# Attention scores as plain fp32 matmuls on paired heads in place of stacked fp32r parts, with one pool of PSUM banks and a new order

## The reference, cut to what matters

```
scores = einsum('bqhd,bkhd->bhqk', q, k) / sqrt(8)    # q = h @ w_q + b_q, k = ctx @ w_k + b_k
attn   = softmax(scores)                              # windowed, full, or over the 16 best keys
o      = einsum('bhqk,bkhd->bqhd', attn, v)           # 16 heads of 8 features
x      = x + gate * (o @ w_o + b_o)
```

## Time and profile before

| what | value |
|---|---|
| runs | 824.49, 845.3, 851.21 us; median 845.3 |
| profiled execution | span 830.0 us from the first to the last instruction; its time outside the span is not listed |
| mean granted clock of TensorE | 0.751 of full speed |
| TensorE matmul busy | 694.1 us, 84% of the span, 5066 instructions |
| VectorE, ScalarE, GpSimd busy | 519.2, 405.8, 240.4 us |
| chain that ended last | TensorE 56%, VectorE 21%, GpSimd 7%, DMA 5% |

### The profile page before, as it was taken

How to read it: one execution, slowest core, us unless ns; L and a number is a source line. 1 busy time by engine, 2 the same in 40 slices (tenths; PEclk the granted TensorE clock), 3 DMA queues, 4 the chain that set the end, 5 groups by cost and what they waited for, 6 DMA issues and landing times.

```text
span 830.0 us, 14443 instructions
## 1 busy us (share of the span) xinstructions
PE 694.1 (84%) x5066; PEld 470.7 (57%) x5066; DVE 519.2 (63%) x1455; ACT 405.8 (49%) x677; POOL 240.4 (29%) x471
## 2 busy tenths in 40 slices
PE   4899997899899898989899887997688968866755
PEld 3675554566566565666566655665555645544533
DVE  3366466635456564646551567778876889899931
ACT  3234555476827476755656570574044713533321
POOL 7511113232333124242112330235010721521302
PEclk9557577798969698969786985597556975886866
DMA  9620203111312401040402060006000220020000
GB/s 346 191 51 3 52 6 65 35 32 23 69 37 52 103 2 43 15 101 8 97 2 53 2 153 1 3 2 145 8 3 1 53 57 3 1 59 0 2 7 6
DMA packets 21700, 39.22 MB, mean 47 GB/s; under 512 B 2496, under 2 KB 6656, under 8 KB 21248
## 3 DMA queue, kind: packets, MB, share of 16 engines
q1 hardware_dynamic: 20912, 37.82, 18.5%
q10 hardware_dynamic: 720, 0.49, 0.2%
HBM read 7.96 MB, written 0.52 MB: 10 GB/s over the span
## 4 chain that ended last, share of the span: by engine, by line
PE 56%; DVE 21%; POOL 7%; DMA 5%; issue 5%; ACT 4%; SPq 2%; POOLq 0%; ACTq 0%; DVEq 0%
PE score L979 14%; PE misc L1025 13%; PE wide L1002 8%; DVE maxima L860 4%; PE wide L1061 4%; DVE left L874 3%; DVE left L882 3%; DVE top L879 3%; PE wide L1036 3%; DVE top L871 3%; DMA qk_stack<-centred 2%; DMA qk_stack<-qk_parts 2%; PE misc L1072 2%; ACT softmax_T L757 2%; SPq L584 2%
## 5 line engine op out<-in xcount | busy, mean ns | idle before, releaser
L860 DVE TENSOR_REDUCE maxima<-score 128x2 f32<-128x512 f32 x320 | 211.8, 687 | 149.0 <-PE score L979 148.0
L757 ACT ACTIVATE softmax_T<-wide 128x1024 f32<-128x1024 f32 (+1 forms) x224 | 211.2, 968 | 106.3 <-PE wide L1002 54.1
L979 PE MATMUL score<-qk_stack 32*128 32x256 f32 (+1 forms) x896 | 215.4, 387 | 53.1 <-DVE maxima L860 20.9
L979 PEld LDWEIGHTS score<-qk_stack 32*128 32x128 f32 x896 | 145.4, 241 | 125.2 <-DVE maxima L860 45.4
L1025 PE MATMUL misc<-softmax_T,values 128*32 128x256 f32 (+1 forms) x1792 | 145.4, 450 | 9.8 <-issue 5.8
L1002 PE MATMUL wide<-qk_stack 32*128 32x256 f32 (+1 forms) x896 | 130.6, 389 | 17.4 <-DMA qk_stack<-centred 9.1
L1002 PEld LDWEIGHTS wide<-qk_stack 32*128 32x128 f32 x896 | 88.3, 240 | 63.4 <-issue 36.3
L686 POOL TENSOR_SCALAR unpicked<-left 128x512 bf16<-128x512 f32 x64 | 39.5, 617 | 191.0 <-DVE left L882 155.1
L1025 PEld LDWEIGHTS misc<-softmax_T,values 128*32 128x32 f32 x1792 | 62.0, 128 | 50.4 <-issue 28.7
L768 ACT ACTIVATE mixed_T<-misc 128x256 f32<-128x256 f32 x112 | 43.6, 389 | 62.0 <-PE misc L1025 61.6
L764 ACT ACTIVATE centred<-misc 16x256 f32<-16x256 f32 (+1 forms) x40 | 14.8, 370 | 104.0 <-PE misc L990 77.8
(11 more groups left out here) (95 smaller groups left out, 802.7 us busy)
## 6 DMA issues: line engine op xcount, KB each, us to landing
qk_stack<-qk_parts SPq DMA_DIRECT2D x112, 256.0 KB, 4.7
weights<-in_w SPq DMA_DIRECT2D x1, 2368.0 KB, 18.3
weights<-in_w SPq DMA_DIRECT2D x1, 1408.0 KB, 13.1
row_biases<-in_rows SPq DMA_DIRECT2D x1, 1088.0 KB, 10.3
weights<-in_w SPq DMA_DIRECT2D x1, 832.0 KB, 8.7
x<-in_x SPq DMA_DIRECT2D x1, 512.0 KB, 4.7
context<-in_ctx SPq DMA_DIRECT2D x1, 512.0 KB, 7.1
out<-x SPq DMA_DIRECT2D x4, 128.0 KB, 2.1
```

What stands on the lines that cost most here:

```text
L757: nc.scalar.activation(pT[:, slot, u % 2, :, 0:cols], wide[:, SLOT["wide", step], :, 0:cols], ACT.Exp).then_inc(fin, 1)
L860: nc.vector.tensor_reduce(rows[:, u // 4, u % 4, :], ps.rearrange("p (t k) -> p t k", t=NT), AX_X, ALU.max).then_inc(fin, 1)
L979: ins = nc.tensor.matmul(ps[:, at:at + (P if window else N)], QKS[b][32 * g:32 * g + 32, s, 0, P * t:P * t + P], QKS[b][32 * g:32 * g + 32 ...
```

## The change

Queries and keys are kept in plain fp32, two heads to a group of 32 rows and 16 rows apart. The parts, the subtraction and the four copies per attention go. The weights of q and k are spread once at the start into planes with the gaps (`pad` on GpSimd), the biases and mask rows come from a 32-row matmul with 512 columns in front of each q and k step. The keys are stored twice, each time with the other head of the pair set to zero (`pair`), so one matmul of 32 rows against 512 columns gives two heads. A score step of a full layer is one such matmul in one bank (still 16 steps); a weights step is four matmuls of 256 columns over two row groups. Both are in plain fp32. The mix of two head groups goes into one bank, so there are two copies and four `divide` transposes in place of four and eight. Maxima go in two halves of 8 heads. All eight banks form one pool; at most two banks may hold scores. The planner's costs, leads and priorities (`BUSY`, `PE_SLOW`, `FIRST`, `LEAD`) are new, and so are all five lists.

```diff
-        parts = sb("qk_parts", [P, SLOTS["qk"], 4, 2, N], F32R)
-        QKS = [sb(f"qk_stack{b}", [P, 4, 2, N], F32R) for b in range(B)]
+        Q = sb("queries", [P, B, 2, N])
+        K = sb("key_pairs", [P, B, 2, 2, N])
...
-        wide = es.enter_context(nc.psum_tensor("wide", [P, 2, 4, N], F32))
-        score = es.enter_context(nc.psum_tensor("score", [P, 2, 512], F32))
-        misc2 = es.enter_context(nc.psum_tensor("misc", [P, 2, 512], F32))
+        banks = es.enter_context(nc.psum_tensor("banks", [P, 8, 512], F32))
...
+SCORES_HOLD, MIX_HOLD = 2, 2
-    ("pe", "scores"): 0.25, ("dve", "scores"): 0.645,
+    ("pe", "scores"): 0.25, ("dve", "scores"): 0.63,
+PE_SLOW = 1.3
-LEAD = (120.0, 80.0, 40.0, 0.0)
+LEAD = (171.0, 120.0, 224.0, 109.0)
...
-                if kind == "stack":
-                    slot = SLOT["qk", ("qk", b, l, 0)]
-                    after(sp, "pool", ("qk", b, l, 0))
-                    sp.dma_start(QKS[b][:, u, :, :].bitcast(F32),
-                                 parts[32 * u:32 * u + 32, slot, :, :, :].bitcast(F32)).then_inc(stacked[b][u], 16)
...
-            nc.vector.memset(parts[:, :, 3, 0, :].bitcast(F32), 0.0).then_inc(q_zero_s, 1)
+            nc.vector.memset(bias_came, 0.0).then_inc(qk_zero_s, 1)
+            nc.vector.memset(wqk[:], 0.0).then_inc(qk_zero_s, 1)      # 3584 columns
...
+                elif kind == "pad":
+                    pool.wait_ge(qk_zero_s, 2)
+                    pool.wait_ge(qk_s[l], 16)
+                    for i in range(2):
+                        ins = nc.gpsimd.tensor_copy(
+                            wqk[:, l, :, :, 4 * i:4 * i + 4, 0:HD].rearrange("p c v s e -> p (c v) s e"),
+                            came[:, l, :, :].rearrange("p c (v s i e) -> p (c v) s i e", v=2, i=2, e=HD)[:, :, :, i, :])
...
+                elif kind == "q":
+                    nc.scalar.activation(Q[:, b, :, :], bank_of(step).rearrange("p (u n) -> p u n", u=2),
+                                         ACT.Copy).then_inc(fin, 1)
+                elif kind == "k":
+                    for j in range(2):
+                        ins = nc.scalar.activation(K[:, b, :, j, :], bank_of(step).rearrange("p (u n) -> p u n", u=2),
+                                                   ACT.Copy, scale=pair[:, j:j + 1])
...
+                        r = 32 * (l % 2 + (0 if kind == "q" else 2))
+                        nc.tensor.matmul(bank, bias_l[r:r + 32, l // 2, :], moving[r:r + 32, :],
+                                         start=True, stop=False)
+                        for i in range(2):
+                            ins = nc.tensor.matmul(bank[:, N * i:N * i + N], 
+                                                   wqk[:, l, 0 if kind == "q" else 1, i, :, :].rearrange("p s e -> p (s e)"), src,
+                                                   start=False, stop=(i == 1))
...
-                            ins = nc.tensor.matmul(ps[:, at:at + (P if window else N)],
-                                                   QKS[b][32 * g:32 * g + 32, s, 0, P * t:P * t + P],
-                                                   QKS[b][32 * g:32 * g + 32, s, 1, keys], start=True, stop=True)
+                        g, v, t = 32 * (u // 4 % 2 * 2 + u % 2), u // 8, u // 2 % 2
+                        ins = nc.tensor.matmul(bank, Q[g:g + 32, b, v, P * t:P * t + P], K[g:g + 32, b, v, :, :],
+                                               start=True, stop=True)
...
+                    for j in range(2):
+                        for t in range(NT) if window else (u % 2,):
+                            for i in range(2):
+                                g = 32 * (2 * (wg % 2) + i)
+                                ins = nc.tensor.matmul(to, K[g:g + 32, b, wg // 2, j, P * t:P * t + P],
+                                                       Q[g:g + 32, b, wg // 2, queries],
+                                                       start=(j == 0 or not topk), stop=not topk)
```

More of the change, by code:

```diff
@@ L149 @@
[L149 to L154, removed]
-}
+    ("pe", "context"): 0.25, ("act", "context"): 0.35,
@@ new lines @@
+    ("pe", "heads_out"): 0.25, ("act", "heads_out"): 0.35, ("pe", "residual"): 0.25, ("dve", "residual"): 0.42,
+    ("pool", "pad"): 0.7, ("pool", "gated"): 0.5, ("pool", "pre"): 1.2,
+    ("pe", "up"): 0.95, ("act", "up"): 1.5, ("pe", "up_gate"): 0.95, ("dve", "up_gate"): 1.75,
+    ("pe", "down"): 0.95, ("dve", "down"): 0.42, ("sp", "store"): 0.7,
+}
+PE_SLOW = 1.3
+FIRST = {"divide": 225.0, "down": -37.0, "heads_out": 35.0, "k": -34.0, "maxima": -20.0, "mix": -88.0,
+         "normed": 26.0, "q": -35.0, "residual": 68.0, "scores": -7.0, "stats": 75.0, "topk": -34.0,
+         "up": 19.0, "values": 136.0, "weights": -19.0}
@@ L156 @@
 LANDS = 2.0
[L157 to L163, removed]
-READER = {"mods": "dve", "gates": "dve", "pbias": "dve", "context": "act", "normed": "act", "qk": "act",
-          "values": "act", "mix": "act", "heads_out": "act", "residual": "dve", "down": "dve", "maxima": "act",
-          "weights": "act", "divide": "dve", "up": "act", "up_gate": "dve", "scores": "dve", "topk": "dve"}
+LATE = 0.25
@@ new lines @@
+HOP = 0.12
+SLOTS = {"pt": 3, "left": 2, "nm": 2}
+BANKS = {k: 1 for k in ("mods", "gates", "pbias", "context", "normed", "q", "k", "values", "mix", "heads_out",
+                        "residual", "down", "maxima", "divide")}
+BANKS["scores"] = 1
+BANKS.update({k: 2 for k in ("topk", "weights", "up", "up_gate")})
+READER = {"mods": "dve", "gates": "dve", "pbias": "dve", "context": "act", "normed": "act", "q": "act",
+          "k": "act", "values": "act", "mix": "act", "heads_out": "act", "residual": "dve", "down": "dve",
+          "maxima": "act", "weights": "act", "divide": "dve", "up": "act", "up_gate": "dve", "scores": "dve",
+          "topk": "dve"}
@@ L188, in plan @@
         pbias_of[l] = task("dve", step, task("pe", step))
+    pad = [task("pool", ("pad", 0, l, 0)) for l in range(7)]
     for b in range(B):
@@ L341, in start_of @@
                 return None
+            if ring == "pt" and len(slots[ring]) == 1:
+                _, b, l, n = t[1]
+                wg = group_of(l, n)
+                if wg % 2 == 0 or ("bank", ("mix", b, l, wg - 1)) not in slot:
+                    return None
             s = max(s, slots[ring][0][0])
@@ L364, in plan @@
         if best is None:
-            raise RuntimeError("the rings are held in a circle")
+            raise RuntimeError("the slots are held in a circle")
         _, s, t = best
@@ L379, in plan @@
         lists[eng].append(step)
+        if eng == "pe":
+            _, got = banks_for(step, s)
+            slot["bank", step] = got[0]
+            had["bank", step] = sorted({reader_of(bank_had[i]) for i in got if bank_had[i]}) \
+                if not (kind == "mix" and u % 2) else []
+            for i in got:
+                bank_at[i], bank_had[i] = None, step
+        else:
+            for i in range(8):
+                if bank_had[i] is not None and bank_at[i] is None and reader_of(bank_had[i]) == t:
+                    bank_at[i] = (s + d / 2 if kind == "topk" else end) + HOP
         ring = takes(t)
@@ L808, in _ @@
                 fin = done[kind, "dve"]
-                misc = misc2[:, SLOT["misc", step], :] if RING.get(kind) == "misc" else None
                 if kind == "mods":
@@ L867, in _ @@
                         after(dve, "pool", HAD["left", step])
-                    if u >= 8 and g == 0:
-                        after(dve, "pe", ("maxima", b, l, u // 4 - 2))
-                    for t in range(NT):
-                        ins = nc.vector.max(top8[:, b, r, g, t, :], ps[:, N * t:N * t + N])
+                    if wg >= 2:
+                        after(dve, "pe", ("maxima", b, l, wg - 2))
+                    for h in range(4):
+                        ins = nc.vector.max(best[:, h, :], ps[:, h, :])
```

717 lines of the change are left out of this document (391 added, 326 removed).

## The result

The changed kernel takes **1056.5 us** (median of four runs, 1047.1 to 1065.5); beside it the kernel before took 841.5 us (four runs, 824.5 to 851.2). The ratio is **1.263, with a 95% interval of 1.231 to 1.296**: slower, as forecast, but by some 210 us and not by 350. The profiled execution took 1048.4 us, with a span of 1046.5 us and a mean granted clock of 0.83.

What follows compares the result with a forecast made beforehand. TensorE bounds the kernel: 521 us-f (busy us times clock) + 148 + 140 + 72 - 7 = 874, less 30 run-out = 844; 844 / 0.75 / 0.95 + 3 = 1188, said 1190 us; range 950 to 1390.

Steps and rivals of the forecast that it cites:

- Scores, +148: TensorE's score matmuls in plain fp32: 91 us-f before, 358 in single file, 239 with pairing, so +148.
- factor of 1.5: TensorE's score steps: assumed pairing of neighbours in different row groups, between 1 and 2; 358/1.5 = 239 us-f.
- Weights, +140: TensorE's weights steps in plain fp32: 48 us-f before, 188 after, so +140.
- factor of 1.9: TensorE's weights steps: divisor for matmuls alternating between two row groups, 91/1.9 = 48 and 358/1.9 = 188 us-f.
- q and k, +72: TensorE's q and k steps with bias matmuls: 0.86 us-f a layer becomes 3.44, over 28 layers +72.
- Total, 844 us-f: TensorE's whole work after the change: 874 us-f summed, less 30 for run-out, gives 844.
- Busy share 95%: TensorE's busy share of the time rises from 84% to 95% through freed latency and the pool of banks.
- Clock, 0.75: TensorE's mean granted clock stays at 0.75, bounds 0.65 and 0.95.
- (1) Full clock: Rival: TensorE never stops and gets the full clock almost throughout, 844 / 0.97 + 3 = 873 us; chance 0.15.
- (2) Several row groups and 770 us: Rival: three or more row groups at once in scores and weights, 656 us-f, clock 0.9, 770 us; chance 0.06.
- (3) Two score banks that stall TensorE: Rival: TensorE's list is stuck behind waiting score steps, +120, 1310 us; chance 0.13 together with single file and low clock.
- (4) Single file and low clock, 1448: Rival: TensorE's scores at +267, clock 0.70, 1448 us; chance 0.13 together with the score-bank stall.

Runs made afterwards that it cites:

- Experiment 1: Kernel before, with scores and weights matmuls reading the same stacked tiles as plain fp32: 1144.2 us, beside 839.9 to 855.0 for the kernel before.
- experiment 10: Changed kernel with four score banks, scores and weights steps ordered across four row groups, and scores, weights and bias in fp32r: 844.9 us, 1.023 of the kernel before.
- experiment 11: Kernel before, with each weights step's four matmuls in row-group order g, g+1, g, g+1: 826.5 us, ratio 1.003.
- experiment 4: Changed kernel with full layers' score steps reordered so that two neighbours share a row group: 1276.3 us.
- experiments 5 and 6: Changed kernel with four score banks and full layers' score steps over four row groups: 968.0 us; then full layers' weights steps alternating row-group pairs too: 951.2 us.

## Why the prediction was right, and where it was off

The direction, the cause and the bound held: TensorE's work sets the end, and plain fp32 makes that work. Experiment 1 has the loss without the rest of the change; experiment 10 has the new lists and the pool, with four score banks, without the loss. Of the signs that the prediction named, these came: two instructions for each score matmul, at least 587 ns for one of 512 columns, 93% busy, VectorE at 49% with its wait for scores on top, no stack copies; TensorE's busy time stayed under 1000 us, at 972.

*Scores, +148.* By line totals times mean clock: 215.4 x 0.751 = 162 before, (255.8 + 29.3 + 45.5) x 0.83 = 274 after, so **+112**. The forecast had 91 and 239, columns alone; a line's total also has the run-out of its steps, which these two lack. Pairs are fewer than the factor of 1.5 took them to be, not more: 358 in single file over 274 is 1.3, and a full-layer step costs 255.8 x 0.83 / 320 = 0.66, between 0.43 (always paired) and 0.86. (With the clock of each moment in place of the mean, the trace gives 156 and 281, +125.) The prediction named score matmuls that start together as a sign against it; as a sign it was badly chosen, since its own factor rested on them.

*Weights, +140.* 130.6 x 0.751 = 98 before, 278.6 x 0.83 = 231 after: **+133**. The factor of 1.9 holds: eight plain fp32 instructions in 1.13 us are two pairs of 0.43 and 0.27 around them, as the four fp32r matmuls in 0.50 us from which it was taken are two pairs of 0.11 and 0.27; experiment 11 and the starts there bear the reading out. Both ends are some 45 above the forecast's 48 and 188, since each step has that 0.27, which drops out of the difference.

*q and k, +72.* Lines 961 and 962 had 46.8 us, 35 us-f; lines 1083 and 1086 have 73.2 + 75.6 = 148.8, 124 us-f: **+88**. The bias line alone is 61 where 56 matmuls of 0.86 make 48; its run-out was not in the sum. (The three rises make more than the whole, 333 for 286, since lines that overlap are counted once in the total.)

*Total, 844 us-f.* Measured 807, 4% less. *Busy share 95%*: measured 93%; of TensorE's 136 idle us before, 1046.5 - 972.4 = 74 are left.

***Clock, 0.75.*** This is the step that failed; it makes 115 of the some 140 us between forecast and time. "Nothing in the stretches says that a busier TensorE has the higher level" was right, and experiment 4 shows it. But "the new steps run on the same engine with the same neighbours" was not: with the score steps in pairs the clock was 0.83, and in single file, with the same lists, 0.70. From the forecast's 844/0.75/0.95 = 1185 the clock takes 115 us (844/0.83/0.95 = 1070), the work 47 (807/0.83/0.95 = 1023), and the busy share gives 23 back (807/0.83/0.93 = 1046). The measured clock lies inside the bounds that the prediction gave (0.65 to 0.95).

*The rivals.* (1) Full clock: part of the way, 0.89 in the first three quarters, and then the last quarter at 0.64. The Trainium skill's rule behind it (TensorE: Matmul & The Clock Gate, section "Why this matters for your kernels"), that a TensorE without gaps runs at full speed, does not hold here: in experiment 4 it had no gap from 400 to 460 us and a clock of 0.58. (2) Several row groups and 770 us: experiments 5 and 6 built it, and got 968 and 951. The clock of 0.88 was near its 0.9; the sum was not, 754 for 656. The Trainium skill's 3.07 times for four row tiles (same page, section "Part 3: Packing small matmuls — row/col tiling") is for tiles that stand together; the score line came to 255.8 x 0.83 / (184.3 x 0.882) = 1.31 times as fast as in pairs. (3) Two score banks that stall TensorE: the idle time before line 1100 is 0.6 us. VectorE waits for the scores for 234 us, as that rival said, but it is VectorE's time, which is not scarce. That rival's 0.2 us for hops stands in no row: in the trace of before a reduce that waits starts 0.04 us after its scores' end, and a weight load that waits 0.05 us after the reduce's (medians). (4) Single file and low clock, 1448: experiment 4 is that rival, 1276, with its clock exactly and less work than it had (841 for 963).

What stays open: why the granted clock goes with the way in which these matmuls stand. The runs show the levels (single file 0.69, pairs 0.89, fours 0.92 in the first stretch; 0.72 and 0.79 for pairs and fours in fp32r) at 88 to 99% busy. Only single file against pairs, and plain fp32 against fp32r, are far apart for runs of one kernel, which differ by up to 0.05 themselves; pairs and fours are not. They don't show what the chip looks at. Nor was the 3 us at the start told apart from the rest.

## What to carry to other kernels

Count a plain fp32 matmul as four fp32r ones of the same columns, also on 32 rows: dropping three-product stacks for plain fp32 took the kernel's DMA traffic from 39.2 to 10.1 MB, where TensorE had waited some 10 us for the copies of the stacks (3.6 + 6.5), and cost 286 us-f on the engine that sets the end. When TensorE is the bound, forecast work and clock apart, and take the clock as a term with bounds of its own: in plain fp32 the order of steps and the banks for scores moved it between 0.70 and 0.88, and the work only from 841 to 754. Where 32-row matmuls of plain fp32 must be used, put steps of different row groups next to each other and give them banks enough; the order of the matmuls within a step of two row groups made no difference here.

## What the runs showed of the hardware that was not expected

- TensorE had 60.00 of 60.00 us busy at a granted clock of 1.00 in one kernel and of 0.58 in another that differs only in which row group follows which.
- Two 512-column plain fp32 matmuls in two row groups took 1.13 us at full clock, one alone 1.12. Four fp32r ones of 256 columns in two row groups took 0.50, two in one row group 0.50; that the code had the four in the order g, g, g+1, g+1 did not keep them from starting in pairs.
- GpSimd takes 797 ns to subtract the mean and multiply, and took 447 ns to add the negated mean and multiply, on a 128 x 128 tile of the same kind. The mean also comes from another tile (`mean_var` for `neg_mean`), so which of the two makes the difference is not shown. The first row is of the changed kernel's groups, the second of those of the kernel before:

```profile
L738 POOL TENSOR_SCALAR centred<-x,mean_var,rstd 128x128 f32<-128x128 f32 x80 | 63.1, 797 | 4.2
```
```profile
L631 POOL TENSOR_SCALAR centred<-x,neg_mean,rstd 128x128 f32<-128x128 f32 x80 | 35.2, 447 | 4.4
```

The change saves the instruction that negates the mean (9.2 us in all) and pays 28 us for it, on an engine with time to spare.
